# Quarter sums among the second layer's tiles, one bias row for two experts, and four PSUM places for second-layer tiles

## The chip, the cores and the metric

The kernel runs on one core of one Trainium2 chip, in one launch. The metric is the device time of that launch in microseconds (us). TensorE is called PE, VectorE DVE, ScalarE ACT, GpSimd POOL and SyncE SP, as in the profile.

## The reference

One layer of a graph transformer over N = 1250 nodes of D = 768 features, in fp32:

```
xn = layernorm(x)
x  = x + gnn(xn, edges) + mix(xn)        # mix: linear attention, then an MLP 768 -> 3072 -> 768 (Gelu)
x  = x + ffn(layernorm(x))               # a router picks 2 of 4 experts, for all nodes alike

def ffn(x):
    gates, (e0, e1) = top-2 softmax of mean(x) @ router_w.T + router_b
    out = sum over e in (e0, e1) of gate_e * (act_e(x @ w1[e] + b1[e]) @ w2[e] + b2[e])   # 768 -> 1536 -> 768
    return layernorm(out + x) * g + b
```

The change concerns the MLP of `mix` and the two experts of `ffn`.

## The kernel before

The 1250 rows are ten tiles of 125 (`NT`, `TP`). An fp32 product is made of three: each operand is split into a high part (rounded to the format PE multiplies) and a low part, and high x high, high x low and low x high are added up in PSUM.

MLP and experts are worked off in **groups** of 128-row blocks of the hidden layer (two blocks, or four in a layer's last group), numbered through: 0 to 10 are the MLP, 11 to 16 the first expert, 17 to 21 the second. A group has two stages on PE:

1. The first layer, transposed, in three chunks of columns (416, 416, 418). It writes PSUM `pb`, four banks. In plain groups (0, 1, 10, 11, 12, 21) it is a job of 18 matmuls per block and chunk (`up_job`, L1243): six jobs for two blocks. The other sixteen are *seven-product* groups (`seven_products`, L1276): a scheme of Strassen's kind over halves of the features and two of the chunks takes nine pieces, 99 matmuls in all, in place of 108. It needs three sums of quarters of the input X, as high and low parts (`T_hi`, `T_lo`), which are made once for the MLP and once for the experts.
2. The second layer, ten token tiles (`down_job`, L1247; `token_tile`, L775, matmuls at L783). Each adds all blocks of the group for 125 rows and 768 columns, 12 matmuls, and writes one of two places in PSUM `pa` (two banks each), `wide(pa, t % 2)`. Tile t waits until the tile two before has been added by DVE (semaphore `dn_acc`), and until the hidden columns it reads are there (`h_lo`).

The other engines:

- ACT (`up`, L2008; `job_out`, L1990; `pair_out`, L2032) applies bias and activation to a job into a ring of three buffers `tr`. In seven-product groups it also copies three partial products (`u_cp`) that DVE needs, and in group f + 1 (f is 0 or 11) makes the high parts of the quarter sums (`high_part`, L2003): the first before the jobs, the second behind job 0, and two after the last job.
- DVE (`hidden`, L2638) splits each job's result into high (L2665) and low part (L2667); in seven-product groups it also adds the partial products (`c_sum`, L2649 to L2655). `down` (L2670) adds each second-layer tile to the token tile `TK` (L2677 in the MLP, L2679 with the gate in the experts). `quarter_sums` (L2682, instructions at L2690) are 13 additions over 128 x 1248 elements, numbered 0 to 12, on two scratch buffers `qs`. Before the change 0 to 4 stand behind tiles 1, 3, 5, 7 and 9 of group f, 5 to 10 behind the six jobs of group f + 1, 11 and 12 behind its tiles 1 and 4.
- DVE adds the experts' output biases to the ten token tiles (`out_bias`, L2796, instructions at L2806), gate times row plus tile, two tiles behind each job from the second on: in group 11 for the first expert, in group 17 for the second.
- POOL splits the weights into high and low parts (L1444, L1445; for seven-product groups also the sums of the weights' quarters, L1527 to L1538). The two second-layer pages of a group (`dw`) are split as soon as the last tile of the group before is done.
- SP's queue loads weight pages into a ring of three raw buffers, each when POOL has split the page before in it, the bias row `b2r` in the first group of each expert (`ffn_b2`, L745), and writes a quarter of X to DRAM (`quarter_out`, L700), which the last quarter sums overwrite in SBUF and the last group reads back.

The order on each engine is written out by hand, and semaphores alone tie the engines together:

```
def down_job(group, t):
    d = NT * group + t
    if d >= 2:
        pe.wait_ge(*at("dn_acc", d - 1))
    pe.wait_ge(*at("h_lo", hidden_of(group, chunk_of(t))))
    token_tile(wide(pa, t % 2), t, ...)
```

Of the kernel before, what the change touches and what calls it, by code (L numbers as in the profile page):

```python
# [8 lines left out]
TP = 125  # L9
NT = N // TP  # L10
# [21 lines left out]
PLAIN = 2  # L32
# [184 lines left out]
def gps_layer(nc, A, out):  # L217
    ctx = ExitStack()
    with ctx:
# [3 lines left out]
        def follow(kind, *parts):  # L223

            before = 0
            for name, n in parts:
# [10 lines left out]
        follow("dve_once", ("e_f", 1), ("e_cmm", 2), ("e_bc", 1), ("bnd", 1), ("ln_v", 1), ("ln_r", 1), ("sn", 2), ("sn2", 1), ("ma0", 1), ("na0", 1), ("sa0", 1), ("ma1", 1), ("na1", 1), ("sa1", 1), ("nl0", 1), ("nl1", 1), ("ev0", 1), ("ev1", 1),  # L237
               ("sn2l", 1), ("kvf", 2),
               ("r_pool", 1), ("r_idx", 1), ("r_d", 1), ("r_gates", 1), ("f_last", 1))
        follow("dve_rows", ("wt_ev", NT), ("g_ev", 2 * NT), ("h2_ev", NT), ("xg_ev", NT), ("kv_ev", 2 * NT), ("l_x1", NT), ("b2_add", 2 * NT), ("f_cn", NT))  # L240

        follow("act_once", ("s_f", 1), ("e_ec", 1), ("v_cp", 1), ("ra0", 1), ("xa0", 1), ("ra1", 1), ("xa1", 1), ("xs_a", NT))
        for q in range(3):
# [248 lines left out]
        def q_slot(r):  # L492

            return (r - QLAST + 2) % QRING

        def edge_sums(t):

            return pb if t == 1 else pa
# [27 lines left out]
        def _(sp):  # L526
# [204 lines left out]
                tile_dma(sp, x2_d[t], x2s[t % 3][:], f"x2_out{t % 3}")  # L731

            sp.wait_ge(*at("r_idx", 1))
            for e in range(TOPK):
                ei_ = sp.value_load(rti[0:1, e:e + 1], min_val=0, max_val=EXP - 1)
                for g in range(len(EXP_SIZES[e])):
                    G_ = expert_group(e, g)
                    for b in range(0 if e or g else 1, SIZES[G_]):
                        m = block_of(G_, b)
                        src = w1e[:, ds(ei_, 1), :, m * P:(m + 1) * P]  # L740
                        block_page(up_page(G_, b), src.rearrange("p e k n -> p (e k) n"))
                    if g == 0:
                        if e:
                            sp.wait_ge(*at("b2_add", NT * e))
                        tile_dma(sp, RW["b2r"][:], A["ffn_b2"][ds(ei_, 1), :].rearrange("e n -> (e n)").partition_broadcast(TP), "b2_in")  # L745
                    if G_ == LASTS[1]:
                        quarter_in(1)
                        sp.wait_ge(*at("b2_add", NT * TOPK))
                        tile_dma(sp, ln_g, A["ffn_ln_g"].partition_broadcast(TP), "gb_in")
                        sp.wait_ge(*at("c_sum", 3 * PAIRS[G_]))  # L750
                        tile_dma(sp, ln_b, A["ffn_ln_b"].partition_broadcast(TP), "gb_in")
                    for k in range(SIZES[G_]):
                        m = block_of(G_, k)
                        src = w2e[:, ds(ei_, 1), m:m + 1, :]
                        page_load(down_page(G_, k), (raw[down_page(G_, k) % NRAW][:], src.rearrange("p e k n -> p (e k n)")))
                    if G_ == MLP_GROUPS:
                        quarter_out(1)
# [16 lines left out]
        def _(pe):  # L774
# [471 lines left out]

            def down_job(group, t):  # L1247

                d = NT * group + t
                if d >= 2:  # L1250
                    pe.wait_ge(*at("dn_acc", d - 1))
                pe.wait_ge(*at("h_lo", hidden_of(group, chunk_of(t))))
                token_tile(wide(pa, t % 2), t, [(hb_hi[k], hb_lo[k]) for k in range(SIZES[group])], dw,
                           [down_page(group, k) for k in range(SIZES[group])]).then_inc(sem("dn_mm"), 1)

            def half_product(bank, slot, half, right, fresh):
# [42 lines left out]
                whole_product(1)  # L1299

            def group_jobs(group, hook=lambda n: None):
                if seven(group):
                    seven_products(group)
                    return
                for n, (b, c) in enumerate(up_order(group)):
                    up_job(group, b, c, JOB0[group] + n)
                    hook(n)
# [272 lines left out]
        def _(act):  # L1580
# [427 lines left out]
            def up(group, func, bias):  # L2008
                build = [s for s, f in enumerate(FIRSTS) if group == f + 1]
                if seven(group):  # L2010
                    pair_out(group, func, bias)
                    return
                for s in build:
                    high_part(s, T_hi[0][:], qs[0], 3)
                for s, last in enumerate(LASTS):
                    if group == last:
                        act.wait_ge(*at("xq_in", 32 * s + 32))
                        for h in range(2):
                            A_(quarter(0, 1)[h], RW[f"xq{h}"][:], ACT.Copy).then_inc(sem("t_hi"), 1)
                for n, (b, c) in enumerate(up_order(group)):  # L2020
                    act.wait_ge(*at("up_mm", PROD0[group] + n + 1))
                    job_out(group, n, func, bias, pb[:, n % 4, 0:CHUNKS[c][1]])
                    for s in build:
                        if n == 0:
                            high_part(s, T_hi[1][:], qs[1], 6)
                for s in build:
                    act.wait_ge(*at("up_mm", PROD0[group + 1]))
                    act.wait_ge(*at("xq_out", 32 * s + 32))
                    high_part(s, quarter(0, 1)[0], qs[0], 9)
                    high_part(s, T_hi[2][:], qs[1], 12)  # L2030
# [79 lines left out]
        def _(dve):  # L2110
# [527 lines left out]
            def hidden(group, mish=None, hook=lambda n: None):  # L2638

                i = PAIRS[group]  # L2640
                for n, (b, c) in enumerate(up_order(group)):
                    j = JOB0[group] + n
                    o, w = CHUNKS[c]
                    z = tr[j % 3][:, 0:w]
                    if seven(group) and n == 0:
                        dve.wait_ge(*at("h_lo", j))
                        dve.wait_ge(*at("up_mm", PROD0[group] + 4))
                        dve.wait_ge(*at("u_cp", 3 * i + 1))
                        v.tensor_tensor(tr[j % 3][:, 0:CP], pb[:, 2, 0:CP], cp[0], ALU.add).then_inc(sem("c_sum"), 1)  # L2649
                        dve.wait_ge(*at("u_cp", 3 * i + 3))  # L2650
                        v.tensor_tensor(tr[(j + 1) % 3][:, 0:CP], pb[:, 1, 0:CP], cp[0], ALU.add).then_inc(sem("c_sum"), 1)
# [18 lines left out]
            def down(group, t, scale=None, out_=None, **kw):  # L2670
# [3 lines left out]
                out_ = tok if out_ is None else out_  # L2674
                dve.wait_ge(*at("dn_mm", d + 1))
                if scale is None:
                    ins = v.tensor_tensor(w2(out_), wide(pa, t % 2), w2(tok), ALU.add)  # L2677
                else:
                    ins = v.scalar_tensor_tensor(out=w2(out_), in0=wide(pa, t % 2), scalar=scale, in1=w2(tok), op0=ALU.mult, op1=ALU.add, **kw)  # L2679
                ins.then_inc(sem("dn_acc"), 1)  # L2680

            def quarter_sums(s, n):  # L2682

# [13 lines left out]
                elif n == 2:  # L2697
                    dve.wait_ge(*at("t_st", first + 2))
                    made(qs[0], qs[0], qs[1], ALU.add)
                elif n == 3:  # L2700
                    dve.wait_ge(*at("t_hi", high + 1))
                    made(T_lo[0][:], qs[0], h1)
                elif n == 4:
                    dve.wait_ge(*at("t_st", first + 4))
                    made(qs[1], d_hi, qs[0])
                elif n == 5:
                    dve.wait_ge(*at("t_st", first + 5))
                    made(qs[1], qs[1], d_lo, ALU.add)
                elif n == 6:
                    dve.wait_ge(*at("t_hi", high + 2))  # L2710
                    made(T_lo[1][:], qs[1], h2)
# [18 lines left out]
            def sums_in_jobs(group):  # L2730

                for s, f in enumerate(FIRSTS):
                    if group == f + 1:
                        return lambda n: quarter_sums(s, 5 + n)
                return lambda n: None

            def sums_in_tiles(group, t):

                for s, f in enumerate(FIRSTS):
                    if group == f and t % 2:  # L2740
                        quarter_sums(s, t // 2)
                    if group == f + 1 and t in (1, 4):
                        quarter_sums(s, 11 + t // 4)

            dve.wait_ge(*at("l_tok", NT))
            for g in range(MLP_GROUPS - 1):
# [46 lines left out]
            dve.wait_ge(*at("r_idx", 1))  # L2793
            ers = [dve.value_load(rti[0:1, e:e + 1], min_val=0, max_val=EXP - 1) for e in range(TOPK)]

            def out_bias(e):  # L2796

                row = RW["b2r"]

                def add(n):  # L2800
                    if n == 1:
                        dve.wait_ge(*at("b2_in", 32 * (e + 1)))
                    for t in range(2 * n - 2, 2 * n) if n else ():
                        if e:
                            dve.wait_ge(*at("dn_acc", NT * (expert_group(1, 0) - 1) + t + 1))
                        v.scalar_tensor_tensor(out=TK[:, t, :], in0=row[:], scalar=gate[0:TP, e:e + 1], in1=TK[:, t, :],  # L2806
                                               op0=ALU.mult, op1=ALU.add).then_inc(sem("b2_add"), 1)
                return add

            def offset(t):  # L2810

                dve.wait_ge(*at(f"X2_in{t // 2}", 64))
# [9 lines left out]
            def expert(e, mish):  # L2822
                for g in range(len(EXP_SIZES[e])):
                    grp = expert_group(e, g)
                    hidden(grp, mish, out_bias(e) if g == 0 else early_offsets if grp == ALL_GROUPS - 1 else sums_in_jobs(grp))
                    if grp < ALL_GROUPS - 1:
                        for t in range(NT):
                            if g == 0:
                                dve.wait_ge(*at("b2_add", NT * e + t + 1))
                            else:  # L2830
                                dve.wait_ge(*at("dn_acc", NT * (grp - 1) + t + 1))
                            down(grp, t, gate[0:TP, e:e + 1])
                            sums_in_tiles(grp, t)

# [57 lines left out]
```

## Time and profile before

| | |
|---|---|
| median of 3 runs | 1972.08 us (1971.07 to 1972.60) |
| the profiled execution, its own time | 1974.13 us |
| its span | 1972.3 us |
| mean granted clock of TensorE | 0.982 |
| instructions | 28809 |
| PE, PEld, DVE, ACT, POOL busy (us) | 1891.2, 1801.0, 1284.3, 651.7, 552.9 |
| first MLP group to last tile of the last group | about 918 to 1965 us |

All later times come from the one profiled execution. PEld is PE's loading of weights, which overlaps its matmuls. "Idle before" names the time an engine stood before an instruction and what released it; "issue" means that the profile shows no releaser. In the views of stretches, PEclk is the mean granted clock of TensorE, 1.00 being 2.4 GHz and 0.50 being 1.2 GHz.

### The profile page before, as it was taken

To read this page: it belongs to the slowest core of one execution; us is meant where nothing else is said; L and a number is where in the kernel's file an instruction comes from. 1 tells how busy PE (TensorE), PEld (TensorE's weight loads), DVE (VectorE), ACT (ScalarE), POOL (GpSimd) and SP (SyncE) were. 2 spreads that over 40 slices of the span, in tenths; PEclk is the share of its full clock that TensorE was granted. 3 is DMA by queue.
4 is the path that set the end of the run, shared out by engine and by line. 5 is a ranking of instruction groups with operands and counts; after the bars stand their busy time and mean duration, and the time that the engine had idled before them with its cause. 6 is when DMAs were issued, how large, how long until landed. Compare 5 with 4: busy or idle time off the path is not lost.

```text
span 1972.3 us, 28809 instructions
## 1 busy us (share of the span) xinstructions
PE 1891.2 (96%) x10837; PEld 1801.0 (91%) x10837; DVE 1284.3 (65%) x2276; ACT 651.7 (33%) x1243; POOL 552.9 (28%) x443
## 2 busy tenths in 40 slices
PE   7999999999899999999999999999988999979998
PEld 4677999999899999899999999999988999979998
DVE  8998679998884324788764445543668545655548
ACT  6534238887784312335111111111421111111113
POOL 1000002110002313144425454542025454535420
PEclk9999999999899999999999999999988999989999
DMA  6332302121245110034011111120331111111314
GB/s 178 113 112 85 115 14 57 43 63 51 85 135 142 58 32 17 17 110 145 18 31 37 44 49 33 33 90 11 103 104 33 33 37 53 33 33 33 106 40 125
DMA packets 83125, 130.67 MB, mean 66 GB/s; under 512 B 7463, under 2 KB 53321, under 8 KB 82991
## 3 DMA queue, kind: packets, MB, share of 16 engines
q1 hardware_dynamic: 78430, 115.58, 20.1%
q10 hardware_dynamic: 4560, 13.31, 2.3%
q8 instruction: 83, 1.36, 0.3%
q14 instruction: 52, 0.42, 0.1%
HBM read 100.86 MB, written 28.01 MB: 65 GB/s over the span
## 4 chain that ended last, share of the span: by engine, by line
PE 79%; DVE 11%; ACT 5%; issue 3%; ACTq 0%; DVEq 0%; SPq 0%; DMA 0%
PE pa L783 23%; PE pb L783 10%; PE pb L1262 9%; PE pb L1243 6%; PE pb L1272 5%; PE pa L849 5%; PE pa L995 4%; PE pb L915 3%; PE pb L1148 3%; PE pa L949 2%; PE pb L995 2%; DVE hl L2667 1%; DVE TK L2806 1%; DVE hh L2665 1%; ACT sm L1741 1%
## 5 line engine op out<-in xcount | busy, mean ns | idle before, releaser
L783 PE MATMUL pa<-dw_hi,hh 128*125 128x384 f32 x960 | 255.5, 348 | 30.4 <-DVE TK L2679 16.9
L783 PE MATMUL pa<-dw_hi,hl 128*125 128x384 f32 x960 | 252.0, 344 | 0.0
L783 PE MATMUL pa<-dw_lo,hh 128*125 128x384 f32 x960 | 252.0, 344 | 0.0
L783 PEld LDWEIGHTS pa<-dw_hi,hh 128*125 128x125 f32 x960 | 176.6, 191 | 38.5 <-DVE TK L2679 20.5
L783 PEld LDWEIGHTS pa<-dw_lo,hh 128*125 128x125 f32 x960 | 177.6, 190 | 0.4
L783 PEld LDWEIGHTS pa<-dw_hi,hl 128*125 128x125 f32 x960 | 177.7, 190 | 0.2
L2679 DVE SCALAR_TENSOR_TENSOR TK<-pa,gate,TK 125x768 f32<-125x768 f32 x110 | 111.5, 1016 | 92.1 <-PE pa L783 91.3
L2677 DVE TENSOR_TENSOR TK<-pa,TK 125x768 f32<-125x768 f32 x100 | 95.6, 956 | 92.5 <-PE pa L783 92.5
L2667 DVE TENSOR_TENSOR hl<-tr,hh 128x416 fp32r<-128x416 f32 x144 | 146.0, 1014 | 4.9
L2665 DVE CAST hh<-tr 128x416 fp32r<-128x416 f32 x144 | 74.1, 514 | 106.7 <-ACT tr L2001 106.7
L2037 ACT ACTIVATE cp<-pb 128x416 f32<-128x416 f32 x32 | 16.6, 518 | 361.4 <-PE pb L1262 361.4
L2001 ACT ACTIVATE tr<-pb,V 128x416 f32<-128x416 f32 (+1 forms) x96 | 58.1, 609 | 217.9 <-PE pb L1243 151.5
L1444 POOL CAST dw_hi<-raw 128x768 fp32r<-128x768 f32 x48 | 42.2, 879 | 287.8 <-PE pa L783 287.8
L849 PE MATMUL pa<-S1h,D1h 125*125 125x418 bf16 x540 | 110.5, 357 | 3.4 <-DVE S1h L2166 3.4
L2166 DVE TENSOR_SCALAR S1h<-iota,ec 125x1254 bf16<-125x1254 f16 x200 | 109.1, 545 | 0.3 <-issue 0.3
L849 PEld LDWEIGHTS pa<-S1h,D1h 125*125 125x125 bf16 x540 | 64.0, 138 | 49.5 <-DVE S1h L2166 37.2
L1243 PE MATMUL pb<-X_hi,uw_hi 128*128 128x416 f32 (+1 forms) x288 | 102.7, 357 | 2.4 <-DVE uw_lo L2782 2.4
L1243 PE MATMUL pb<-X_lo,uw_hi 128*128 128x416 f32 (+1 forms) x288 | 102.2, 355 | 0.0
L1243 PE MATMUL pb<-X_hi,uw_lo 128*128 128x416 f32 (+1 forms) x288 | 102.2, 355 | 0.0
L995 PE MATMUL pa<-G,PT 125*125 125x193 f32 (+1 forms) x580 | 92.4, 316 | 0.0
L1445 POOL TENSOR_TENSOR dw_lo<-raw,dw_hi 128x768 fp32r<-128x768 f32 x48 | 90.8, 1891 | 3.9
L949 PE MATMUL pa<-ident,sm 125*125 125x125 f32 x580 | 77.9, 283 | 12.7 <-ACT sm L1741 10.1
(465 smaller groups left out, 4650.7 us busy)
## 6 DMA issues: line engine op xcount, KB each, us to landing
raw<-in_L_mix_fc_w SPq DMA_DIRECT2D x48, 384.0 KB, 3.4
raw<-in_L_ffn_w SPq DMA_DIRECT2D x47, 384.0 KB, 3.3
md<-md_d SPq DMA_DIRECT2D x11, 546.9 KB
md_d<-mds SPq DMA_DIRECT2D x10, 546.9 KB
raw<-in_L_mix_qkv_w SPq DMA_DIRECT2D x24, 192.0 KB, 4.3
md<-md_d ACTq DMA_DIRECT2D x8, 546.9 KB
TOK<-in_x SPq DMA_DIRECT2D x10, 336.0 KB
xn_d<-TOK SPq DMA_DIRECT2D x10, 336.0 KB
```

The costliest lines, as they stand in the source:

```text
L783: last = nc.tensor.matmul(slot[:, c, :], x_[:, cols], w_[:, c * HD2:(c + 1) * HD2], start=(k == 0 and n == 0), stop=(k == len(blocks) - 1 ...
L849: last = nc.tensor.matmul(acc[0:TP, c, 0:CH], RM[f"D1h{q}"][:], RM[f"S1h{q}"][:, c * CH:(c + 1) * CH], start=False, stop=True, skip_group_ ...
L949: last = nc.tensor.transpose(pa[0:TP, q, (j - a) * TP:(j - a + 1) * TP], sm[i % 3][:, columns(j)], ident[0:TP, 0:TP])
L995: last = nc.tensor.matmul(sums(i)[0:TP, 0:n], RX[f"PT{i % 2}"][:, columns(j)], rows, start=(j == 0), stop=(j == NT - 1))
L1243: last = nc.tensor.matmul(pb[:, (j - JOB0[group]) % 4, 0:n], w_[:, kk, :], x_[:, kk, o:o + n], start=(kk == 0 and q == 0), stop=(kk == KT ...
L1262: last = nc.tensor.matmul(pb[:, bank, 0:CP], w_[:, HW * half + kk, :], x_[:, kk, :], start=(fresh and kk == 0 and q == 0), stop=(kk == HW ...
L1272: last = nc.tensor.matmul(pb[:, 3, 0:n], w_[:, kk, :], x_[:, kk, o:o + n], start=(kk == 0 and q == 0), stop=(kk == KT - 1 and q == 2))
L2166: v.tensor_scalar(RM[f"S1h{q}"][:], RM["iota"][:], ec[:, ds(first + (q % 2) * EW, 1)], None, ALU.is_equal).then_inc(sem(f"oh{q}"), 1)
L2665: v.tensor_copy(hb_hi[b][:, o:o + w], z).then_inc(sem("h_hi"), 1)
L2667: v.tensor_tensor(hb_lo[b][:, o:o + w], z, hb_hi[b][:, o:o + w].bitcast(fp32), ALU.subtract).then_inc(sem("h_lo"), 1)
L2677: ins = v.tensor_tensor(w2(out_), wide(pa, t % 2), w2(tok), ALU.add)
L2679: ins = v.scalar_tensor_tensor(out=w2(out_), in0=wide(pa, t % 2), scalar=scale, in1=w2(tok), op0=ALU.mult, op1=ALU.add, **kw)
```

## The change

- The quarter sums are put elsewhere. Numbers 3, 4 and 5 change places with each other (the first low part is now number 5). In group f the six sums 0 to 5 stand behind tiles 1, 3, 5, 6, 8 and 9. In group f + 1 only two stand behind jobs (6 behind job 1, 7 behind job 4), and 8, 9, 10 and 11 behind tiles 0, 2, 4 and 6. Number 12 stands at the start of group f + 2. ACT makes both high parts of the first two sums before group f + 1's first job.
- The two experts' bias rows are loaded together in group 11, one into `b2r`, the other into the buffer `spare`; DVE makes gate0 x row0 + gate1 x row1 of them behind jobs 1 and 2, and adds this row to the ten token tiles at the start of groups 13, 14, 15 (three each) and 16 (one). Nothing is left of it in group 17.
- Second-layer tiles use four places, two in `pa` and two in `pb`; group 10 keeps two. A tile waits for the one that had its place before, tile 2 also for the last activation of the group's first layer, and the next group's first layer for tile 7 (it writes the same banks of `pb`).

```
+        def down_slot(group, t):
+            if group == LASTS[0]:
+                return wide(pa, t % 2)
+            return wide((pa, pa, pb, pb)[t % 4], t % 2)
+        def down_before(group, t):
+            if group == LASTS[0]:
+                return NT * group + t - 2
+            return NT * group + t - 4 if t >= 4 else NT * (group - 1) + (8, 9, 6, 7)[t]
@@ sync @@
+            eis = [sp.value_load(rti[0:1, e:e + 1], min_val=0, max_val=EXP - 1) for e in range(TOPK)]
             for e in range(TOPK):
-                ei_ = sp.value_load(rti[0:1, e:e + 1], min_val=0, max_val=EXP - 1)
+                ei_ = eis[e]
...
-                    if g == 0:
-                        if e:
-                            sp.wait_ge(*at("b2_add", NT * e))
-                        tile_dma(sp, RW["b2r"][:], A["ffn_b2"][ds(ei_, 1), :].rearrange("e n -> (e n)").partition_broadcast(TP), "b2_in")
+                    if e + g == 0:
+                        sp.wait_ge(*at("c_sum", 3 * PAIRS[MLP_GROUPS]))
+                        for i_, row in zip(eis, (RW["b2r"][:], RZ["spare"][0:TP, :])):
+                            tile_dma(sp, row, A["ffn_b2"][ds(i_, 1), :].rearrange("e n -> (e n)").partition_broadcast(TP), "b2_in")
                     if G_ == LASTS[1]:
                         quarter_in(1)
-                        sp.wait_ge(*at("b2_add", NT * TOPK))
+                        sp.wait_ge(*at("b2_add", 2 + NT))
@@ tensor @@
             def down_job(group, t):
-                d = NT * group + t
-                if d >= 2:
-                    pe.wait_ge(*at("dn_acc", d - 1))
+                if down_before(group, t) >= 0:
+                    pe.wait_ge(*at("dn_acc", down_before(group, t) + 1))
+                if t == 2:
+                    pe.wait_ge(*at("up_act", JOB0[group + 1]))
                 pe.wait_ge(*at("h_lo", hidden_of(group, chunk_of(t))))
-                token_tile(wide(pa, t % 2), t, [(hb_hi[k], hb_lo[k]) for k in range(SIZES[group])], dw,
+                token_tile(down_slot(group, t), t, [(hb_hi[k], hb_lo[k]) for k in range(SIZES[group])], dw,
...
             def group_jobs(group, hook=lambda n: None):
+                if group not in FIRSTS:
+                    pe.wait_ge(*at("dn_acc", NT * (group - 1) + 8))
@@ scalar @@
                 for s in build:
                     high_part(s, T_hi[0][:], qs[0], 3)
+                    high_part(s, T_hi[1][:], qs[1], 5)
...
-                    for s in build:
-                        if n == 0:
-                            high_part(s, T_hi[1][:], qs[1], 6)
@@ vector: hidden @@
                     if seven(group) and n == 0:
+                        for s, f in enumerate(FIRSTS):
+                            if group == f + PLAIN:
+                                quarter_sums(s, 12)
+                        if group > MLP_GROUPS:
+                            out_bias(group)
                         dve.wait_ge(*at("h_lo", j))
@@ vector: down reads down_slot(group, t) instead of wide(pa, t % 2) @@
+            def bias_row(n):
+                row = RW["b2r"][:]
+                if n == 1:
+                    dve.wait_ge(*at("b2_in", 64))
+                    v.tensor_scalar(row, row, gate[0:TP, 0:1], None, ALU.mult).then_inc(sem("b2_add"), 1)
+                if n == 2:
+                    dve.wait_ge(*at("b2_add", 1))
+                    v.scalar_tensor_tensor(out=row, in0=RZ["spare"][0:TP, :], scalar=gate[0:TP, 1:2], in1=row,
+                                           op0=ALU.mult, op1=ALU.add).then_inc(sem("b2_add"), 1)
+            def out_bias(group):
+                first = 3 * (PAIRS[group] - PAIRS[MLP_GROUPS])
+                for t in range(first, min(first + 3, NT)):
+                    dve.wait_ge(*at("b2_add", 2))
+                    dve.wait_ge(*at("dn_acc", NT * (group - 1) + t + 1))
+                    v.tensor_tensor(TK[:, t, :], TK[:, t, :], RW["b2r"][:], ALU.add).then_inc(sem("b2_add"), 1)
@@ vector: sums_in_jobs, sums_in_tiles @@
                     if group == f + 1:
-                        return lambda n: quarter_sums(s, 5 + n)
+                        return lambda n: quarter_sums(s, {1: 6, 4: 7}.get(n))
...
-                    if group == f and t % 2:
-                        quarter_sums(s, t // 2)
-                    if group == f + 1 and t in (1, 4):
-                        quarter_sums(s, 11 + t // 4)
+                    if group == f:
+                        quarter_sums(s, {1: 0, 3: 1, 5: 2, 6: 3, 8: 4, 9: 5}.get(t))
+                    if group == f + 1:
+                        quarter_sums(s, {0: 8, 2: 9, 4: 10, 6: 11}.get(t))
@@ vector: expert @@
-                    hidden(grp, mish, out_bias(e) if g == 0 else early_offsets if grp == ALL_GROUPS - 1 else sums_in_jobs(grp))
+                    hidden(grp, mish, bias_row if e + g == 0 else early_offsets if grp == ALL_GROUPS - 1 else sums_in_jobs(grp))
                     if grp < ALL_GROUPS - 1:
                         for t in range(NT):
-                            if g == 0:
-                                dve.wait_ge(*at("b2_add", NT * e + t + 1))
-                            else:
+                            if e + g:
                                 dve.wait_ge(*at("dn_acc", NT * (grp - 1) + t + 1))
+                            if seven(grp) and t == 0:
+                                dve.wait_ge(*at("b2_add", 2 + min(3 * (PAIRS[grp + 1] - PAIRS[MLP_GROUPS]), NT)))
                             down(grp, t, gate[0:TP, e:e + 1])
```

## Rows read from the trace of the kernel before

**Rows 1.** the page: busy time by engine, costliest group, a DMA issue

```profile
PE 1891.2 (96%) x10837; PEld 1801.0 (91%) x10837; DVE 1284.3 (65%) x2276; ACT 651.7 (33%) x1243; POOL 552.9 (28%) x443
...
L783 PE MATMUL pa<-dw_hi,hh 128*125 128x384 f32 x960 | 255.5, 348 | 30.4 <-DVE TK L2679 16.9
...
raw<-in_L_ffn_w SPq DMA_DIRECT2D x47, 384.0 KB, 3.3
```

**Rows 2.** stretches: us, then busy of PE, PEld, DVE, ACT, POOL, PEclk, DMA, GB/s

```profile
961.29:1013.11 51.82, 46.51 (x229) 45.54 (x229) 39.44 (x31) 7.17 (x9) 26.68 (x16) 0.90 0.10 31
961.29:981.90 20.61, 20.53 (x108) 19.90 (x107) 16.95 (x11) 4.12 (x7) 19.84 (x13) 1.00 0.12 38
1032.03:1053.47 21.44, 21.44 (x121) 21.07 (x121) 11.10 (x11) 0.61 (x1) 12.27 (x10) 1.00 0.13 37
1461.00:1488.16 27.16, 23.14 (x121) 22.80 (x122) 21.58 (x24) 1.86 (x2) 0.00 (x0) 0.94 0.00 1
1488.16:1541.23 53.07, 46.49 (x229) 45.53 (x229) 41.56 (x31) 7.17 (x9) 26.66 (x16) 0.90 0.10 30
1541.23:1581.65 40.42, 40.36 (x220) 39.70 (x220) 20.58 (x25) 5.32 (x9) 20.19 (x16) 1.00 0.14 40
1702.91:1760.36 57.45, 44.08 (x220) 43.15 (x220) 36.94 (x35) 6.37 (x10) 23.74 (x16) 0.88 0.10 28
```

**Rows 3.** PE's timeline, where it stood: start, us, what, [idle before <-releaser]

```profile
1469.46 1.00 PE L783 MATMUL pa<-dw_hi,hh 128*125 128x384 f32 x2 [3.85 <-DVE TK L2679]
...
1512.16 0.58 PE L783 MATMUL pa<-dw_hi,hh 128*125 128x384 f32 x2 [3.47 <-issue]
...
1521.25 1.00 PE L783 MATMUL pa<-dw_hi,hh 128*125 128x384 f32 x2 [3.11 <-DVE TK L2679]
...
1741.19 1.00 PE L783 MATMUL pa<-dw_hi,hh 128*125 128x384 f32 x2 [9.91 <-DVE TK L2679]
```

**Rows 4.** the chain of waits in order of time: start, us, what

```profile
1541.23 8.57 PE pb L1262 x45
```

**Rows 5.** DVE's timeline, groups 11 to 13 and 17

```profile
1455.44 1.94 DVE L2806 SCALAR_TENSOR_TENSOR TK<-b2r,gate,TK 125x768 f32<-125x768 f32 x2
...
1475.50 1.02 DVE L2679 SCALAR_TENSOR_TENSOR TK<-pa,gate,TK 125x768 f32<-125x768 f32 x1 [1.08 <-PE pa L783]
1476.43 1.45 DVE L2690 TENSOR_TENSOR qs<-X_lo 128x1248 f32<-128x1248 f32 x1
...
1489.20 3.10 DVE L2690 TENSOR_TENSOR qs<-X_hi,qs 128x1248 f32<-128x1248 f32 x1
...
1493.25 2.12 DVE L2667 TENSOR_TENSOR hl<-tr,hh 128x416 fp32r<-128x416 f32 x1
...
1499.17 0.91 DVE L2665 CAST hh<-tr 128x416 fp32r<-128x416 f32 x1 [1.81 <-ACT tr L2001]
...
1502.15 2.27 DVE L2690 TENSOR_TENSOR T_lo<-qs,T_hi 128x1248 fp32r<-128x1248 f32 x1
...
1548.18 0.59 DVE L2649 TENSOR_TENSOR tr<-pb,cp 128x416 f32<-128x416 f32 x1 [5.82 <-PE pb L1262]
...
1715.28 4.10 DVE L2806 SCALAR_TENSOR_TENSOR TK<-b2r,gate,TK 125x768 f32<-125x768 f32 x2
```

**Rows 6.** POOL's and ACT's timelines, groups 11 and 13

```profile
1544.89 1.84 POOL L1445 TENSOR_TENSOR dw_lo<-raw,dw_hi 128x768 fp32r<-128x768 f32 x1
...
1482.25 1.25 ACT L2006 ACTIVATE T_hi<-qs 128x1248 fp32r<-128x1248 f32 x1 [20.62 <-DVE qs L2690]
...
1549.83 0.52 ACT L2037 ACTIVATE cp<-pb 128x416 f32<-128x416 f32 x1 [0.29 <-PE pb L1262]
```

**Rows 7.** SP's queue after the router's result

```profile
1436.26 0.40 SPq L271 DMA_DIRECT2D b2r<-in_L_ffn_b  x1
```

**Rows 8.** DVE's timeline in the last group's tiles

```profile
1937.46 1.01 DVE L2679 SCALAR_TENSOR_TENSOR TK<-pa,gate,TK 125x768 f32<-125x768 f32 x1
...
1941.64 1.01 DVE L2679 SCALAR_TENSOR_TENSOR TK<-pa,gate,TK 125x768 f32<-125x768 f32 x1
```

More of the change, by code:

```diff
@@ L239, in gps_layer @@
                ("r_pool", 1), ("r_idx", 1), ("r_d", 1), ("r_gates", 1), ("f_last", 1))
-        follow("dve_rows", ("wt_ev", NT), ("g_ev", 2 * NT), ("h2_ev", NT), ("xg_ev", NT), ("kv_ev", 2 * NT), ("l_x1", NT), ("b2_add", 2 * NT), ("f_cn", NT))
+        follow("dve_rows", ("wt_ev", NT), ("g_ev", 2 * NT), ("h2_ev", NT), ("xg_ev", NT), ("kv_ev", 2 * NT), ("l_x1", NT), ("b2_add", 2 + NT), ("f_cn", NT))
         follow("act_once", ("s_f", 1), ("e_ec", 1), ("v_cp", 1), ("ra0", 1), ("xa0", 1), ("ra1", 1), ("xa1", 1), ("xs_a", NT))
@@ L2676, in down @@
                 if scale is None:
-                    ins = v.tensor_tensor(w2(out_), wide(pa, t % 2), w2(tok), ALU.add)
+                    ins = v.tensor_tensor(w2(out_), down_slot(group, t), w2(tok), ALU.add)
                 else:
-                    ins = v.scalar_tensor_tensor(out=w2(out_), in0=wide(pa, t % 2), scalar=scale, in1=w2(tok), op0=ALU.mult, op1=ALU.add, **kw)
+                    ins = v.scalar_tensor_tensor(out=w2(out_), in0=down_slot(group, t), scalar=scale, in1=w2(tok), op0=ALU.mult, op1=ALU.add, **kw)
                 ins.then_inc(sem("dn_acc"), 1)
+            def bias_row(n):
[13 more added lines that the diff above has]
+                    v.tensor_tensor(TK[:, t, :], TK[:, t, :], RW["b2r"][:], ALU.add).then_inc(sem("b2_add"), 1)
             def quarter_sums(s, n):
@@ L2700, in quarter_sums @@
                 elif n == 3:
+                    dve.wait_ge(*at("t_st", first + 3))
+                    made(qs[1], d_hi, qs[0])
+                elif n == 4:
+                    dve.wait_ge(*at("t_st", first + 4))
+                    made(qs[1], qs[1], d_lo, ALU.add)
+                elif n == 5:
                     dve.wait_ge(*at("t_hi", high + 1))
                     made(T_lo[0][:], qs[0], h1)
[L2703 to L2708, printed above, removed]
                 elif n == 6:
@@ L2794, in _ @@
             ers = [dve.value_load(rti[0:1, e:e + 1], min_val=0, max_val=EXP - 1) for e in range(TOPK)]
[L2796 to L2808, printed above, removed]
             def offset(t):
```

## The prediction

> **What bounds the kernel now.** The page first: TensorE (PE) is busy 96% of the span, VectorE (DVE) 65%, and the largest group of matmuls, the second layers' at L783, stood idle 30.4 us, mostly for DVE's L2679 [rows 1]. So PE sets the time, and only time in which PE stands or crawls can be won. The stretches tell where that is [rows 2]. A seven-product group with nothing else in it takes 40.42 us (18.9 for its products, 21.44 for its ten second-layer tiles), and PE is busy 40.36 of them; a plain group's six jobs take 20.61. Against this stand four slow stretches: group 1 (51.82 us), the second layer of group 11 (27.16), group 12 (53.07) and group 17 (57.45). PE's own timeline shows how [rows 3]: in group 12 it waits 3.47 us before the first tile ("issue"; DVE has not yet written the hidden columns), does two tiles, and waits 3.11 more for DVE to add up tile 0. This second wait is 3.85 us in group 11 and 9.91 in group 17. The granted clock of the four is 0.88 to 0.94, against 1.00 in the clean one [rows 2]: after a wait PE works for a while at its lower level (1.2 GHz), so a wait costs more than its own length. The chain of waits goes through PE alone from the end of such a stretch on [rows 4].
>
> Why DVE is late shows in its timeline [rows 5]. In groups 1 and 12 it does six quarter sums between the jobs while POOL splits weights (busy 19.84 of 20.61 us [rows 2]): a sum then takes 2.27 or even 3.10 us in place of 1.45, a low part 2.12. In groups 11 and 17 ten bias additions stand between the jobs: a pair takes 1.94 us, beside POOL 4.10.
>
> **The change, part by part.** S is the moment at which PE starts a group.
>
> (a) Quarter sums. Group f (0 or 11) gets six sums among its tiles instead of five. POOL is idle there (0.00 busy in group 11 [rows 2]), so ten additions and six sums are 10 x 1.02 + 6 x 1.45 = 18.9 us of the 21.44 that PE needs. The last sum, after tile 9, ends at about S + 4.4 of the next group if it is stretched to 3.10 as now. In group f + 1 two sums stay between the jobs instead of six. I follow DVE there at the stretched prices, 3.0 us for a job (0.9 high part, 2.12 low part) and 2.27 for a sum; job 1 is ready at S + 7.5, later ones do not hold DVE up. Job 0 ends at 7.4, job 1 at 10.5, a sum at 12.8, job 2 at 15.8, job 3 at 18.8, where PE wants it at 20.6; job 4 at 21.8, a sum at 24.1, job 5 at 27.1. Tile 0 is added at 28.1; PE wants its place four tiles on, at 20.61 + 4 x 2.14 = 29.2. With sums of 1.45 after tiles 0, 2, 4 and 6, tile 1 is added at 30.6 (wanted at 31.3) and tile 7 at 41.0; the next products want that at 42.05. Every margin is positive, 0.7 to 3 us, so group f + 1 runs at PE's rate, 20.61 + 21.44 = 42.05. Worth 51.82 - 42.05 = 9.8 and 53.07 - 42.05 = 11.0 us. ACT makes the second high part before its first job; its sum ends after tile 8, about S + 0.4, and 1.25 us more [rows 6] are over before the first job is (S + 3.4). The last sum moves into group f + 2, where DVE stands idle 5.82 us for PE's products [rows 5]; PE needs it at the fifth product, S + 6.9, and it ends by S + 1.1 + 2.27 = S + 3.4. Nothing is paid.
>
> (b) Biases. Two instructions in group 11 make one row (1.0 us each, as one of an undisturbed pair), in place of ten additions there: 9.7 us become 2. DVE then ends job 5 about 1.7 us after PE does, and no tile waits. Group 11's second layer: 27.16 - 21.44 = 5.7 us won. Group 17 loses all ten and becomes a clean pair: 57.45 - 40.42 = 17.0 us. Ten additions of the finished row go, 3 + 3 + 3 + 1, into the same 5.82 us of idleness in groups 13 to 16. There POOL splits the two second-layer pages until S + 5.5 [rows 6]. The trace has no plain addition of two SBUF tiles in that place; the bounds are 0.97 (half the 1.94 pair) and 2.05 (half the 4.10 pair). I take 2.05, since POOL works there. Groups 14 and 15: 1.1 + 3 x 2.05 = S + 7.2, against S + 6.95, where DVE now begins its first sum over the products: 0.3 late. Group 13 has the last quarter sum too: 1.1 + 2.27 + 6.15 = S + 9.5, 2.6 late. What hangs on it is ACT's third copy, done at S + 9.1 now [rows 6] and wanted by the seventh product at S + 12.0: 2.9 us of cover. So nothing is paid, with 0.3 us left in group 13; past that each us of DVE is one of PE. POOL's splits are wanted only by the tiles at S + 18.9.
>
> (c) Four places. Tile t waits for tile t - 4 instead of t - 2. In a clean group this buys nothing: PE stands 0.06 us there. Two waits are new. Tile 2 waits for ACT's last activation, half a us or so behind the last product (a copy of that width takes 0.52 [rows 6]), while PE has two tiles, 4.3 us, to do. And each group's products wait until tile 7 of the group before is added; in a clean group DVE is 1.1 us behind PE, which still has two tiles to do: 3.2 us of cover. All of PE's later work is queued behind this wait; it costs nothing while DVE is less than 3.2 us late.
>
> (d) DMAs. On SP's queue a second register read comes before the first expert's second up page, and two bias rows before its down pages, where there was one; the second expert's row, and SP's wait for DVE ahead of it, go. The row was issued at 1436.26 [rows 7] and is read at 1455.44 [rows 5]; a load about as large, a weight page, lands in 3.3 us [rows 1], so one more load of that kind is covered by 15 us. The down pages behind it are wanted at 1461. Nothing.
>
> (e) The end. Group 21 has four places too, but there DVE is the slower one: its additions follow each other every 4.18 us [rows 8], with its other work between, no slower than PE's 24 matmuls of a tile (2 x 2.14). Nothing won.
>
> Here a rule of the Trainium skill speaks against the change. The page "TensorE: Matmul & The Clock Gate", section "A second HAM failure mode: psum-queue depth-cycling", says that cycling through PSUM banks can leave small gaps between groups of matmuls, so that the clock swings between its levels. The clean group cycles through two places at a granted clock of 1.00 [rows 2]: going by the row, four cost nothing; going by the rule, second layers could crawl.
>
> **Sum.** 9.8 + 5.7 + 11.0 + 17.0 = 43.5 us. The profiled execution took 1974.13 us (span 1972.3); against it this makes 1930.6. It lies 2 us above the median of the runs shown, 1972.08; from there 1928.6.
>
> **Rivals.** (1) Margins too thin. If a few DVE instructions of groups 1, 12 or 13 meet POOL worse than now (3.10 for a sum instead of 2.27), PE waits 1 to 4 us in each of the three, and crawls at half speed afterwards for about as long: 3 to 15 us back, 1932 to 1944. For it: DVE is as good as full from S to S + 41 in groups 1 and 12. Against: fewer sums beside POOL let POOL finish sooner too. Chance 0.14.
> (2) Slower, by the new wait for tile 7 ahead of the products of 20 groups. It decides once DVE is over 3.2 us behind there; to eat 43.5 us it must cost 2.2 in each, so DVE would have to lag by 5.4 us in clean groups, where an addition takes 1.02 of every 2.14 us and it catches up. Time then 1973 to 1985. Chance 0.02.
> (3) The clock. Were second layers to fall to the lower level, each could take up to twice its 21.44 us, and two such eat the gain: 1950 to 2000. The clean rows, 1.00 with two places already, speak against. Chance 0.02.
> The clock page's rule named above is the one that would bring this about.
> (4) Nothing changes, since the lateness comes from something else, such as late pages: 1972. Against: both waits of a slow stretch end with DVE's work. Chance 0.01.
>
> **Numbers.** The forecast has 0.81. Its own range is 1926 to 1932: the runs shown scatter by 1.5 us, and a price misjudged by a us or two in one group would show on top. To hold 8 in 10 the range takes in the better half of the first rival: 1925.5 to 1938. A measurement of this kernel tells some 0.2% (4 us) from no change. Faster 0.96 (forecast, first rival, part of the third), same 0.01, slower 0.03.
>
> **What would show it.** Groups 1 and 12 at 42 us, group 17 at 40.4, group 11's tiles in 21.4; granted clock 1.00 in all four; no wait of PE over 1 us for DVE's additions; DVE's 5.82 us of idleness at the start of groups 13 to 15 down to 2 or less, and ACT's third copy in group 13 before S + 12. Wrong if PE waits at a group's first product or before tile 2, if the clock falls in a second layer, or if group 13's first sum over the products comes after S + 10.

## The result, and the profile after

The changed kernel takes 1924.32 us (median of 4 runs, 1921.88 to 1926.73) against 1971.57 beside it: a ratio of 0.9761, 95% interval 0.9744 to 0.9778. That is 47 us less where 43.5 were forecast, and 1.2 us below the stated range. The profiled execution took 1925.01 us, with a span of 1923.2 us and a mean granted clock of 0.991 (0.982 before).

The page of the changed kernel, the lines that answer to [rows 1]. The second layers' matmuls are now in two groups, by `pa` and `pb`; the line is L796 there.

```profile
PE 1871.5 (97%) x10837; PEld 1788.5 (93%) x10837; DVE 1282.7 (67%) x2268; ACT 651.3 (34%) x1243; POOL 553.9 (29%) x443
...
L796 PE MATMUL pa<-dw_hi,hh 128*125 128x384 f32 x608 | 157.4, 340 | 0.7 <-ACT tr L2017 0.7
```

The idle time ahead of the group, 30.4 us before, is 0.7 (and 0.0 ahead of the `pb` group, by the view of lines), and DVE is no longer its releaser. The same stretches as in [rows 2]: group 1, group 2 (clean), the tiles of group 11, group 12, group 13 (now with a quarter sum and three additions in it), group 17.

```profile
960.39:1002.13 41.74, 41.74 (x230) 41.40 (x229) 36.10 (x30) 7.39 (x9) 25.07 (x16) 1.00 0.13 38
1002.13:1042.26 40.13, 40.13 (x221) 39.79 (x220) 21.35 (x26) 5.31 (x9) 21.53 (x16) 1.00 0.13 40
1448.58:1469.78 21.20, 21.20 (x121) 21.15 (x121) 16.52 (x17) 1.86 (x2) 0.00 (x0) 1.00 0.01 1
1469.78:1511.52 41.74, 41.74 (x230) 41.41 (x229) 39.91 (x30) 7.40 (x9) 25.02 (x16) 1.00 0.13 38
1511.52:1551.64 40.12, 40.12 (x221) 39.78 (x220) 29.12 (x29) 5.15 (x9) 22.39 (x16) 1.00 0.14 40
1672.00:1712.12 40.12, 40.12 (x221) 39.78 (x220) 20.82 (x25) 6.48 (x10) 20.43 (x16) 1.00 0.14 40
```

Every one is at a granted clock of 1.00, and PE stands in none of them. The surprise is in the plain numbers: a clean group takes 40.12 us, not the 40.36 (MLP) or 40.42 (experts) of before, and the ten tiles 21.20, not 21.44. The accounts of both profiled executions, in us, each group from the start of its first matmul record (the stretches of groups above and in [rows 2] begin some 0.17 us later):

| part | before | after | less by | forecast |
|---|---|---|---|---|
| group 0 | 43.28 | 43.28 | 0.0 | 0 |
| group 1 | 51.83 | 41.74 | 10.1 | 9.8 |
| groups 2 to 9 | 322.91 | 320.96 | 1.9 | 0 |
| group 10 | 101.95 | 101.73 | 0.2 | 0 |
| group 11 | 50.19 | 44.96 | 5.2 | 5.7 |
| group 12 | 53.06 | 41.74 | 11.3 | 11.0 |
| groups 13 to 16 | 161.68 | 160.48 | 1.2 | 0 |
| group 17 | 57.46 | 40.12 | 17.3 | 17.0 |
| groups 18 to 20 | 121.26 | 120.36 | 0.9 | 0 |
| group 21 and the end | 90.84 | 90.88 | 0.0 | 0 |
| sum | | | 48.2 | 43.5 |

The stretch ahead of group 0, which nothing in the change touches, took 917.84 and 916.95 us in these two executions and between 913.85 and 918.25 in those of the experiments below. That scatter of some 4.4 us is why the accounts go by stretches, not by totals.

### The profile page after: what moved, and what is told of

Same layout as the page of the kernel before. It is cut to its first block, busy times and chain, and to the rows that moved or that the text cites. A ratio compares the mean times of both kernels' runs of the same rounds, so it can differ in the third digit from the quotient of the medians.

```text
span 1923.2 us, 28799 instructions
## 1 busy us (share of the span) xinstructions
PE 1871.5 (97%) x10837; PEld 1788.5 (93%) x10837; DVE 1282.7 (67%) x2268; ACT 651.3 (34%) x1243; POOL 553.9 (29%) x443
## 4 chain that ended last, share of the span: by engine, by line
PE 86%; DVE 5%; ACT 5%; issue 3%; ACTq 0%; DVEq 0%; DMA 0%
PE pb L796 19%; PE pa L796 17%; PE pb L1276 10%; PE pb L1256 9%; PE pb L1286 6%; PE pa L862 5%; PE pa L1008 4%; PE pb L928 3%; PE pb L1161 3%; PE pa L962 3%; PE pb L1008 2%; ACT sm L1757 1%; PE pb L804 1%; PE pb L1039 1%; ACT o1h L1783 1%
## 5 line engine op out<-in xcount | busy, mean ns | idle before, releaser
L796 PE MATMUL pa<-dw_hi,hh 128*125 128x384 f32 x608 | 157.4, 340 | 0.7 <-ACT tr L2017 0.7
L796 PE MATMUL pa<-dw_hi,hl 128*125 128x384 f32 x608 | 156.9, 339 | 0.0
L796 PE MATMUL pa<-dw_lo,hh 128*125 128x384 f32 x608 | 156.7, 339 | 0.0
L796 PEld LDWEIGHTS pa<-dw_hi,hh 128*125 128x125 f32 x608 | 109.8, 186 | 1.5 <-ACT tr L2017 1.1
L796 PEld LDWEIGHTS pa<-dw_lo,hh 128*125 128x125 f32 x608 | 109.8, 186 | 0.4
L796 PEld LDWEIGHTS pa<-dw_hi,hl 128*125 128x125 f32 x608 | 109.9, 185 | 0.2
L2698 DVE SCALAR_TENSOR_TENSOR TK<-pa,gate,TK 125x768 f32<-125x768 f32 x66 | 66.9, 1015 | 42.7 <-PE pa L796 41.9
L796 PE MATMUL pb<-dw_hi,hl 128*125 128x384 f32 x352 | 90.6, 338 | 0.0
L796 PE MATMUL pb<-dw_hi,hh 128*125 128x384 f32 x352 | 90.6, 338 | 0.0
```

Of the source, the lines that this page charges most:

```text
L796: last = nc.tensor.matmul(slot[:, c, :], x_[:, cols], w_[:, c * HD2:(c + 1) * HD2], start=(k == 0 and n == 0), stop=(k == len(blocks) - 1 ...
L2698: ins = v.scalar_tensor_tensor(out=w2(out_), in0=down_slot(group, t), scalar=scale, in1=w2(tok), op0=ALU.mult, op1=ALU.add, **kw)
```

## The experiments

The parts of the change, four **places**, the new order of the **sums** and the one row of **biases**, can be taken apart. Each single part and each pair of them ran, beside the kernels with none and with all.

**Two places again.** Sums and biases as changed.

```
             def down_slot(group, t):
-                if group == LASTS[0]: return wide(pa, t % 2)
-                return wide((pa, pa, pb, pb)[t % 4], t % 2)
+                return wide(pa, t % 2)
...
             def down_before(group, t):
-                if group == LASTS[0]: return NT * group + t - 2
-                return NT * group + t - 4 if t >= 4 else NT * (group - 1) + (8, 9, 6, 7)[t]
+                return NT * group + t - 2
...
             def down_job(group, t):
...
-                if t == 2:
-                    pe.wait_ge(*at("up_act", JOB0[group + 1]))
...
             def group_jobs(group, hook):
-                if group not in FIRSTS:
-                    pe.wait_ge(*at("dn_acc", NT * (group - 1) + 8))
```

> The changed kernel with two places again (both in pa), quarter sums and biases as changed. Theory (what the forecast missed is the place: in each clean group tile 2 waits for tile 0, which DVE adds late): clean groups take 40.36 to 40.42 us instead of 40.12, so 15 x 0.27 = 4 us; groups 1 and 12, where DVE adds tile 0 at S + 27 and tile 2 wants its place at S + 24.8, take 44 to 46 instead of 41.74, so 5 to 9 us more. About 1935, from 1931 to 1939. Rival (the clean groups gained from something else, the sums or biases): clean groups stay at 40.12 and the time is below 1931.

Measured: 1937.02 us (1935.86 to 1938.42), ratio 0.9829 (0.9813 to 0.9846), 12.7 us above the changed kernel. Its stretches: group 1, group 3 (clean), group 12, group 15 (clean), group 17.

```profile
958.37:1004.49 46.12, 43.52 (x229) 42.86 (x229) 36.51 (x30) 7.39 (x9) 25.04 (x16) 0.96 0.12 35
1044.86:1085.22 40.36, 40.36 (x220) 39.71 (x220) 19.98 (x25) 5.31 (x9) 20.21 (x16) 1.00 0.14 40
1474.05:1519.92 45.87, 43.27 (x230) 42.65 (x229) 40.31 (x30) 7.40 (x9) 24.98 (x16) 0.96 0.12 35
1601.11:1641.53 40.42, 40.36 (x220) 39.70 (x220) 27.02 (x28) 5.20 (x9) 21.54 (x16) 1.00 0.13 40
1681.95:1722.38 40.43, 40.37 (x220) 39.71 (x220) 20.81 (x25) 6.48 (x10) 20.42 (x16) 1.00 0.14 40
```

The clean groups are back at 40.36 and 40.42 with the sums and biases out of the way, so it is the places that bought the 0.24 to 0.30 us. The rival falls. In groups 1 and 12 PE's timeline has one wait of 2.60 us, for tile 0, and the clock is 0.96: two places cost 4.4 and 4.1 us there, the wait and some 1.5 to 1.8 more at the lower clock.

```profile
1501.55 1.00 PE L792 MATMUL pa<-dw_hi,hh 128*125 128x384 f32 x2 [2.60 <-DVE TK L2690]
```

Where does a clean group of two places lose its 0.24 us, if PE is busy all the time? Not in the rows of PE but in those of its weight loads. First the loads of group 2 in the kernel before, then DVE in the same group.

```profile
1035.55 0.36 PEld L783 LDWEIGHTS pa<-dw_hi,hl 128*125 128x125 f32 x2
1036.23 0.29 PEld L783 LDWEIGHTS pa<-dw_hi,hh 128*125 128x125 f32 x2 [0.32 <-DVE TK L2677]
```

```profile
1033.19 2.11 DVE L2667 TENSOR_TENSOR hl<-tr,hh 128x418 fp32r<-128x418 f32 x1
1035.23 0.95 DVE L2677 TENSOR_TENSOR TK<-pa,TK 125x768 f32<-125x768 f32 x1
```

The first load of tile 2 stands 0.32 us for the addition of tile 0. DVE cannot begin it before 1035.23, because the group's last low part lasts 2.11 us; it ends at 1036.18, and the load follows at once. The matmul record spans over the gap, since its end is modelled. With four places the loads at that spot, now into `pb`, have no gap:

```profile
1024.57 0.36 PEld L796 LDWEIGHTS pa<-dw_hi,hl 128*125 128x125 f32 x2
1024.92 0.36 PEld L796 LDWEIGHTS pb<-dw_hi,hh 128*125 128x125 f32 x2
```

The Trainium skill has a rule for this reading: its page "Perfetto Trace Analysis", section "Identifying the Most-Contended Engine", says that the busy share of matmuls, which are pipelined, is no good measure of how close a kernel is to the limit, and goes by the busy share of the weight loads and the share of peak arithmetic instead. The trace agrees as far as the loads go: PE was busy 40.36 us of 40.36 while PEld stood 0.32.

**Two places, and POOL held back.** If the late addition comes from POOL, whose second weight split runs beside that low part, it should be enough to hold POOL back.

```
             def pair_split(group):
...
                     pool.wait_ge(*at("up_mm", slot_before(group, s)))
+                    if s == 1 and seven(group - 1):
+                        pool.wait_ge(*at("h_lo", JOB0[group]))
```

> As two_places, and POOL's second split of the next group's weights waits for DVE's last low part of the group. Theory (tile 0 is added late because that low part runs beside POOL, 2.1 us instead of 0.59): with the low part at 0.59 the clean groups take 40.12 with two places too, 3 to 4 us below two_places. Rival (two places cost 0.24 us by themselves, through the order of the waits): clean groups stay at 40.36 to 40.42.

Measured: 1931.61 us (1931.50 to 1934.41), ratio 0.9800 (0.9784 to 0.9816), 5.4 us below two_places. Groups 3 and 9, then groups 15 and 20; behind groups 9 and 20 no pair is split, so the added wait doesn't act in them:

```profile
1045.94:1086.06 40.12, 40.12 (x220) 39.78 (x220) 18.48 (x25) 5.31 (x9) 19.98 (x16) 1.00 0.14 40
1286.66:1327.02 40.36, 40.36 (x220) 39.70 (x220) 19.98 (x25) 7.70 (x11) 16.24 (x12) 1.00 0.28 91
1600.79:1640.91 40.12, 40.12 (x220) 39.78 (x220) 25.52 (x28) 5.20 (x9) 21.32 (x16) 1.00 0.14 40
1801.39:1841.81 40.42, 40.36 (x220) 39.70 (x220) 20.59 (x25) 7.70 (x11) 16.23 (x12) 1.00 0.34 110
```

With two places and POOL held back the clean group takes 40.12 us, as with four; the two groups that the wait doesn't reach stay at 40.36 and 40.42. DVE's last low part is 0.59 us there, and it then waits 0.52 us for PE instead of the other way round:

```profile
1066.11 0.59 DVE L2680 TENSOR_TENSOR hl<-tr,hh 128x418 fp32r<-128x418 f32 x1
1067.23 0.96 DVE L2690 TENSOR_TENSOR TK<-pa,TK 125x768 f32<-125x768 f32 x1 [0.52 <-PE pa L792]
```

So the cause is shown from both ends: two more places hide the late addition, and a POOL that stays away removes it. In groups 1 and 12 PE's wait stays, 2.61 us in each, since there the quarter sums make DVE late; they take 44.56 us, at a granted clock of 1.00, and 45.99, at 0.96.

**The old order of the sums,** four places and the new bias row. The last lines of this diff and of the next tell the tables and calls in short, sum by sum.

```
                 for s in build:
                     high_part(s, T_hi[0][:], qs[0], 3)
-                    high_part(s, T_hi[1][:], qs[1], 5)
...
                     job_out(group, n, func, bias, pb[:, n % 4, 0:CHUNKS[c][1]])
+                    for s in build:
+                        if n == 0:
+                            high_part(s, T_hi[1][:], qs[1], 6)
...
-    group f:      {1: 0, 3: 1, 5: 2, 6: 3, 8: 4, 9: 5}  behind tiles
+    group f:      {1: 0, 3: 1, 5: 2, 7: 3, 9: 4}  behind tiles
-    group f + 1:  {1: 6, 4: 7} behind jobs, {0: 8, 2: 9, 4: 10, 6: 11} behind tiles, 12 in group f + 2
+    group f + 1:  5 + n behind job n, {1: 11, 4: 12} behind tiles
```

> Four places and the new bias row, but the quarter sums where they were. Theory (each part removes its own wait): PE still waits 3.5 us before the first tile of groups 1 and 12, for the hidden columns, and runs slowly after it; the second wait, for tile 0, is gone, since four tiles on it is there. Groups 1 and 12 take 46 to 47 us each (41.74 as changed, 51.8 and 53.1 before), the time is 1933 to 1936. Rival (the sums alone carry all of the gain in these groups): 51 to 53 each, 1944 or more.

Measured: 1934.65 us (1932.42 to 1937.84), ratio 0.9821 (0.9805 to 0.9837). Group 12 in the stretches, and PE's one wait in it:

```profile
1471.73:1518.79 47.06, 43.52 (x230) 42.87 (x230) 39.70 (x31) 7.17 (x9) 26.73 (x16) 0.96 0.12 34
```

```profile
1495.97 0.58 PE L796 MATMUL pa<-dw_hi,hh 128*125 128x384 f32 x2 [3.54 <-issue]
```

As expected: group 1 takes 47.02, group 12 47.06. Of the two waits of group 12 in [rows 3] the first, for the hidden columns, stays; the second, for tile 0, is gone with the places.

**The old biases,** four places and the new sums.

```
-    hidden(grp, mish, bias_row if e + g == 0 else ...)      # 2 instructions in group 11
-    if group > MLP_GROUPS: out_bias(group)                  # 3 + 3 + 3 + 1 additions, groups 13 to 16
+    hidden(grp, mish, out_bias(e) if g == 0 else ...)       # 10 additions in group 11, 10 in group 17
```

> Four places and the new sums, but ten additions of bias in group 11 and ten in group 17. Theory: group 11 costs nothing (DVE adds tile 0 7.4 us into the tiles, with four places it is wanted at 8.6); group 17 waits 3.5 us for the hidden columns and some 7 more for tile 0 at tile 4, so it takes 51 to 54 us instead of 40.12. Time 1935 to 1939. Rival (four places hide the additions in both): under 1929; rival (places do not help here): 1947, 6 us in group 11 and 17 in group 17.

Measured: 1937.91 us (1937.57 to 1939.94), ratio 0.9836 (0.9819 to 0.9852). Group 11's tiles and group 17, then PE's second wait in group 17:

```profile
1448.49:1469.76 21.27, 21.27 (x120) 21.22 (x121) 21.20 (x24) 1.64 (x2) 0.00 (x0) 1.00 0.01 1
...
1671.98:1724.63 52.65, 44.38 (x220) 43.46 (x220) 36.79 (x35) 6.37 (x10) 23.77 (x16) 0.90 0.10 31
```

```profile
1710.47 1.00 PE L796 MATMUL pa<-dw_hi,hh 128*125 128x384 f32 x2 [4.80 <-DVE TK L2696]
```

With the old biases four places are enough to remove the wait of group 11 (21.27 us for the tiles), and they shorten the 9.91 us of group 17 to 4.80; its first wait, 3.46 us for the hidden columns, stays. There the additions had to go.

**Four places alone.** The last two edits together, so that only the places (and SP's earlier register read) are left of the change.

> The kernel before with four places only; sums and biases where they were. Theory (the parts add up as the single ones say, groups 1 and 12 at 47.0 as in old_sums, 17 at 52.7 as in old_biases, group 11's tiles at 21.2, clean groups at 40.12): 1924.3 + 10.3 + 13.6 = 1948, 23 to 24 us below before. Rival (four places help only where sums and biases are out of the way): over 1955.

Measured: 1947.73 us (1946.04 to 1950.32), ratio 0.9889 (0.9873 to 0.9906). Groups 1 and 12 take 47.01 each, group 17 53.13, group 11's tiles and those of the clean groups 21.2. The sum of the single readings (1948) holds.

**The bias row alone,** with two places and the old sums.

> The kernel before with the new bias row only; two places, old sums. Theory: group 11's tiles 21.3 instead of 26.8 and group 17 40.4 instead of 57.5, all else as before: 22.5 us below before, about 1949. Group 13, where the ten additions begin, may lose 0.4 as in two_places. Rival (needs the places): group 17 over 42.

Measured in a single run: 1947.69 us. Group 11's tiles take 21.21, group 17 40.42; group 1 stays at 51.82 and group 12 is at 50.42, 2.6 less than before, with nearly the same two waits (3.54 and 3.11 us; 3.47 and 3.11 before) at a granted clock of 0.97 instead of 0.90: the clock, and not the waits, makes the difference. Group 13 loses nothing here (40.42; in two_places it took 40.77).

**The sums alone,** with two places and the old biases.

> The kernel before with the new order of the quarter sums only; two places, old biases. Theory: groups 1 and 12 at 46.1 and 45.9 as in two_places, instead of 51.8 and 53.1: 12.9 us below before, about 1959; groups 11 and 17 as before. Rival: above 50 in both.

Measured in a single run: 1961.33 us, some 2 above what was expected. Group 1 takes 47.39 and group 12 44.86 (46.12 and 45.87 in two_places), with waits of 2.61 and 2.68 us at 0.93 and 1.00: after nearly equal waits the clock costs between 0.4 us (44.86 less 41.74 less 2.68) and 3.0. Groups 11 and 17 stay slow (26.76 for the tiles, 56.97).

**All ten additions in group 13.** This puts a price on DVE's idle time, in which the change has them three by three.

```
             def out_bias(group):
-                first = 3 * (PAIRS[group] - PAIRS[MLP_GROUPS])
-                for t in range(first, min(first + 3, NT)):
+                for t in range(NT) if PAIRS[group] == PAIRS[MLP_GROUPS] else ():
...
                             if seven(grp) and t == 0:
-                                dve.wait_ge(*at("b2_add", 2 + min(3 * (PAIRS[grp + 1] - PAIRS[MLP_GROUPS]), NT)))
+                                dve.wait_ge(*at("b2_add", 2 + NT))
```

> The changed kernel with all ten additions of the bias row at the start of group 13 instead of 3 + 3 + 3 + 1. Theory (what is put into DVE's idle time is free up to ACT's third copy, wanted at S + 12.0): seven more additions of 0.87 us bring DVE's first sum over the products from S + 8.9 to S + 15.0 and the copy to S + 16.9, so PE waits 4.9 us before the seventh product of group 13 and runs slowly for a while: group 13 takes 45 to 48 us instead of 40.12, the time is 5 to 8 us above the changed kernel's 1924.3. Rival (DVE and PE are looser than that): group 13 stays within 1 us of 40.12.

Measured: 1933.89 us (1933.20 to 1935.33), ratio 0.9817 (0.9801 to 0.9833), 9.6 us above the changed kernel. Group 13 takes 49.88 us, at a clock of 0.90. DVE's ten additions and what follows, then PE's wait:

```profile
1514.11 13.27 DVE L2717 TENSOR_TENSOR TK<-TK,b2r 125x768 f32<-125x768 f32 x10
1527.30 0.58 DVE L2668 TENSOR_TENSOR tr<-pb,cp 128x416 f32<-128x416 f32 x1
```

```profile
1529.20 0.68 PE L1276 MATMUL pb<-X_hi,uw_hi 128*128 128x416 f32 x1 [7.14 <-ACT cp L2051]
```

The mechanism is the one named: PE waits for ACT's third copy, ahead of the seventh product. The size was under-estimated, 4.9 us of wait against 7.14: undisturbed additions follow each other every 0.87 us, as expected, but two of the later ones meet POOL's next split (from 1522.13 on) and last 1.57 and 2.55 us instead of 0.94, which is 2.2 us more. At the lower clock another 2.6 us are lost.

## Why the prediction was right or wrong

**Right: where the time was, and what would remove it.** The four slow stretches gave 9.8, 5.7, 11.0 and 17.0 us on paper and 10.1, 5.2, 11.3 and 17.3 in the trace. The sign holds, and no rival came: in the four stretches PE waits neither at a group's first product nor before tile 2, and the clock is 1.00. (Group 11's first product waits 2.36 us behind the router, before and after alike.) The experiments show that the effects overlap: taken away alone, the places cost 12.7 us, the sums 10.3 and the biases 13.6; alone, they bring 23, 9 and 23, the last two by single runs. The places and the biases both pay for groups 11 and 17, and the places and the sums share the two waits of groups 1 and 12.

**Wrong: step (c), "in a clean group this buys nothing: PE stands 0.06 us there".** It bought 0.24 us in each of eight MLP groups and 0.30 in each of seven expert groups, 4.0 us together, and 0.3 us more in each of the slow groups 1, 12 and 17, for which I had taken tiles of 21.44 us as the best there is. That is 4.9 us of the 48.2 (group 11 fell 0.5 short and group 10 gained 0.2), and without it the time would lie inside the range. The mistake was one of reading: the 40.36 us of busy PE in [rows 2] have modelled ends and cover a short wait; the row of the weight loads shows it. The lower bound stood on the scatter of the runs and a us or two for one group's price, with no look at how a gain in the clean groups could arise. Of the 6.3 us between the forecast 1930.6 and the measured 1924.3, another 2.0 come from the starting point, the profiled execution's 1974.13 instead of the median 1972.08; that is the scatter of single runs.

**Step (a), the margins.** DVE's course in group 12 can be held against the forecast, with S at 1469.78.

```profile
1490.01 3.10 DVE L2728 TENSOR_TENSOR qs<-X_hi,qs 128x1248 f32<-128x1248 f32 x1
...
1494.05 2.12 DVE L2686 TENSOR_TENSOR hl<-tr,hh 128x418 fp32r<-128x418 f32 x1
1496.10 1.00 DVE L2698 SCALAR_TENSOR_TENSOR TK<-pa,gate,TK 125x768 f32<-125x768 f32 x1
...
1508.05 1.00 DVE L2698 SCALAR_TENSOR_TENSOR TK<-pb,gate,TK 125x768 f32<-125x768 f32 x1
...
1512.56 3.10 DVE L2728 TENSOR_TENSOR T_lo<-qs,T_hi 128x1248 fp32r<-128x1248 f32 x1
1515.58 4.96 DVE L2718 TENSOR_TENSOR TK<-TK,b2r 125x768 f32<-125x768 f32 x3
1520.46 0.58 DVE L2668 TENSOR_TENSOR tr<-pb,cp 128x416 f32<-128x416 f32 x1
```

Tile 0 is added at S + 27.3 (forecast 28.1), tile 7 at S + 39.3 (41.0). A sum between the jobs did take 3.10 us instead of 2.27, as the first rival feared, but other instructions beside POOL came out cheaper than the prices taken. In group 13 (S at 1511.52) the last quarter sum took 3.10 instead of 2.27 and the three additions 1.65 each instead of 2.05; the first sum over the products starts at S + 8.9, forecast S + 9.5, and ACT's third copy ends at S + 10.7, before the S + 12.0 at which it is wanted. In group 14 three additions took 6.61 us, 2.2 each, and the sum starts at S + 7.6, forecast S + 7.2. All of it was covered, as forecast, and the last experiment shows that the cover ends where it was said to end.

**Step (b).** Of the two instructions in group 11 one is cheaper than forecast (0.61 us, the scaling of one row), the other as forecast (1.01). The tiles of group 11 gained 5.6 us, near the forecast 5.7 by two errors that nearly cancel: from their first matmul they took 26.83 us, while the stretch of 27.16 began too early, at 1461.00; and they came down to 21.20 us, not 21.44. The jobs of group 11 lost 0.4, at the lower clock behind the router, which is scatter: 22.98 to 24.32 us in the executions shown.

**Steps (d) and (e)** cost and gave nothing, as said: the two rows were issued from 1423.69 on and first used at 1444.53, and the end took 90.88 us against 90.84. That "DVE is the slower one" in group 21 was wrong, though nothing hung on it: PE was busy 42.29 us in the 43 from 1922.50 on before the change, DVE 37.23.

**The clock.** Four places in turn didn't make it fall: 1.00 in every group from 1 to 9 and from 12 to 20. In these groups of all the kernels shown it stood below 1.00 only where PE had waited 2.6 us or more at a time, and not in all of those: group 12 of sums_alone and group 1 of two_places_pool_waits stayed at 1.00. The short wait of 0.32 us in the clean groups left it there. The rule of the Trainium skill that was held against the change, on cycling through PSUM banks ("TensorE: Matmul & The Clock Gate", the section on psum-queue depth-cycling), does not show itself here.

## What to carry to other kernels

To see whether the bound engine really never waits, read the rows of its weight loads, and compare equal stages with each other (group 0's tiles took 21.20 us before the change, the clean ones 21.44): an identical stage that is faster somewhere is a wait elsewhere. A second buffer is enough only while its consumer is on time. Here the consumer was late by one instruction, a low part that takes 2.11 us beside POOL and 0.59 without, and two more places hid that in all stages at once. Work moved into idle time of a side engine is free up to a point that can be named beforehand, the instruction that the bound engine wants next.

## What the runs showed of the hardware that had not been expected

The price of a wait through the clock is not fixed: nearly the same pair of waits (3.47 and 3.11 us; 3.54 and 3.11) made group 12 take 53.06 us in one execution and 50.42 in another, and single waits of 2.60 to 2.68 us cost between 0.2 us (group 1 of two_places_pool_waits: 44.56 less 41.74 less 2.61) and 3.0 on top of themselves. A matmul record can cover a real wait of 0.3 us, as shown above. And an addition of two SBUF tiles takes 0.95 us in the end of the kernel, where POOL is idle, and follows the one before after 0.87 in a row of them; beside POOL's splits single ones of the bias additions took 1.57 to 2.60 us. POOL's split grew beside them too: in group 14 its second high part took 1.56 us and the low part behind it 2.44, against 0.82 and 1.84 in group 13 before the change.
